# A two-layer transformer on one core: expert results stored by indirect transfers in token order, and cross attention reordered

## The reference, cut to what matters

```python
x = x + ga * _L0_attn_ref(layernorm(x) * (1 + ca) + sa)
x = x + gb * _L0_ffn_ref(layernorm(x) * (1 + cb) + sb)      # 8 experts, top 2
x = x + ga * _L1_attn_ref(...)                              # 16 heads of 8
x = x + gb * _L1_ffn_ref(...)     # cross attention over the batches, then 8 experts, top 2
...
scores = jnp.einsum('sbhd,tbhd->bhst', q, k) * scale        # s, t: 4 batches
attn = jnp.einsum('bhst,tbhd->sbhd', jax.nn.softmax(jnp.where(causal, scores, ...)), v)
...
expert_out = jnp.einsum('etf,efh->eth', gelu(jnp.einsum('th,ehf->etf', x, moe_w1)), moe_w2)
moe_out = jnp.einsum('eth,et->th', expert_out, weights)     # weights: 0 but for the best 2
```

## Time and profile before

| what | us |
|---|---|
| median of 3 runs (2000.09 to 2002.37) | 2000.48 |
| the profiled execution, its own time | 1998.0 |
| span of the profile, first to last instruction | 1996.2 |
| busy: PE, DVE, ACT, POOL | 1524.6, 1306.7, 1121.0, 544.4 |

### The profile page before, as it was taken

One profiled execution on the slowest core, in us unless ns is written; L12 is line 12 of the kernel. 1 busy time (PEld: TensorE's weight loads), 2 busy tenths in 40 slices (PEclk: granted clock), 3 DMA queues, 4 the chain that ended last, 5 costly groups with the idle time before them and its releaser, 6 DMA issues. The chain is left out here.

```text
span 1996.2 us, 36212 instructions
## 1 busy us (share of the span) xinstructions
PE 1524.6 (76%) x12536; PEld 846.8 (42%) x12536; DVE 1306.7 (65%) x3285; ACT 1121.0 (56%) x2869; POOL 544.4 (27%) x614
## 2 busy tenths in 40 slices
PE   6799999999924994338999999999999635414910
PEld 3377777777724994221222222222222324414910
DVE  5655656666651321669999999999999268833423
ACT  3377777777712442343888888888888533201300
POOL 1143334536255003731001001001000020471056
PEclk8799999999966997666999999999999957556955
DMA  6155212112105772340000000000000000014822
GB/s 207 38 175 182 88 32 52 42 39 56 32 28 169 228 228 86 90 134 17 23 20 25 19 27 19 27 18 27 18 19 2 1 6 1 22 51 137 263 80 71
DMA packets 86208, 139.61 MB, mean 70 GB/s; under 512 B 18084, under 2 KB 57252, under 8 KB 85772
## 3 DMA queue, kind: packets, MB, share of 16 engines
q1 hardware_dynamic: 62860, 92.60, 15.7%
q0 software_dynamic: 11936, 34.49, 5.2%
q10 hardware_dynamic: 11232, 10.23, 1.5%
HBM read 76.03 MB, written 45.11 MB: 61 GB/s over the span
## 5 line engine op out<-in xcount | busy, mean ns | idle before, releaser
L2064 DVE TENSOR_REDUCE q_max<-s_ps 128x1 f32<-128x1024 f32 x512 | 597.8, 1217 | 14.2 <-PE s_ps L1955 6.5
L2045 ACT ACTIVATE probs<-s_ps 128x512 f32<-128x512 f32 x1024 | 535.5, 603 | 124.4 <-PE s_ps L1976 124.2
L1955 PE MATMUL s_ps<-k_stack,q_stack 64*128 64x512 bf16 x1024 | 351.4, 396 | 17.0 <-PEq L97 8.6
L1976 PE MATMUL s_ps<-q_stack,k_stack 64*128 64x512 bf16 x1024 | 319.6, 384 | 20.1 <-ACT probs L2045 15.7
L1990 PE MATMUL o_ps<-probs,v_aug 128*32 128x512 f32 x2048 | 273.6, 606 | 0.7 <-ACT probs L2045 0.7
L1976 PEld LDWEIGHTS s_ps<-q_stack,k_stack 64*128 64x128 bf16 x1024 | 78.4, 94 | 334.5 <-ACT probs L2045 282.4
L873 ACT ACTIVATE probs<-s_biased,s_min 128x128 f32<-128x128 f32 x512 | 198.8, 391 | 15.8 <-DVE s_min L962 14.5
L991 POOL TENSOR_TENSOR probs<-probs,p_rsum 128x512 f32<-128x512 f32 x128 | 132.7, 1037 | 270.3 <-DVE p_rsum L968 269.8
L962 DVE CUSTOM_DVE_ANT_0 s_biased<-score_ps,nbias 128x128 f32<-128x128 f32 x512 | 117.7, 285 | 48.9 <-PE score_ps L738 37.1
L1582 POOL CAST neg_max_parts<-neg_max 16x128 bf16<-16x128 f32 x32 | 9.0, 281 | 474.6 <-DVE neg_max L2072 474.6
L974 DVE COPY probsT<-probsT_ps 128x512 f32<-128x512 f32 x128 | 86.9, 679 | 71.4 <-PE probsT_ps L750 71.4
(11 more groups left out here) (313 smaller groups left out, 2683.6 us busy)
## 6 DMA issues: line engine op xcount, KB each, us to landing
moe0b_wblock<-in_L_ffn_blocks SPq DMA_DIRECT2D x39, 578.0 KB, 4.1
moe_rows<-zero_rows POOLq DMA_DIRECT2D x18, 960.0 KB, 4.8
moe1b_wblock<-in_L_ffn_blocks SPq DMA_DIRECT2D x39, 256.0 KB, 3.6
v_shift<-v_tiles SPq DMA_DIRECT2D x32, 256.0 KB
v_shift<-v_tiles SPq DMA_DIRECT2D x32, 224.0 KB
qk_parts_dram<-qk_parts SPq DMA_DIRECT2D x16, 384.0 KB, 2.7
q_stack<-qk_parts_dram SPq DMA_DIRECT2D x192, 32.0 KB
k_stack<-qk_parts_dram SPq DMA_DIRECT2D x192, 32.0 KB
```

What stands on the lines that cost most here:

```text
L1955: mm = nc.tensor.matmul(s1[u % 2][:, c * CH:(c + 1) * CH], qs[head_rows(m), quad % 4, j, qt * P:(qt + 1) * P], ks[head_rows(m), quad % 4, ...
L1976: nc.tensor.matmul(bank_of("exp", 4 * k + pos)[:], ks[head_rows(m), quad % 4, j, kt * P:(kt + 1) * P], qs[head_rows(m), quad % 4, j, half ...
L2045: nc.scalar.activation(pr[:, k % 2, HEADS[pos], :], bank_of("exp", n)[:], ACT.Exp).then_inc(sm["exp"], 1)
L2064: v.tensor_reduce(mx[:, h % 4, col:col + 1], s1[u % 2][:], AX.X, ALU.max).then_inc(sm["maxed"], 1)
```

## The change

Four things are changed.

1. **Tags.** A row that is scattered now has 130 elements: the 128 features, the token's number (t+1)/4096, and the first row of the span of its first expert (`tag`, three small DVE instructions a batch, in `choose`). Each layer has its own `moe_rows`, both cleared during window attention: 36 transfers on POOL's queue in place of 18.
2. **Results in token order.** In `block_stage` DVE works out from the two tags where each row of a block belongs (`destinations`, three instructions of 128x2): the token's place in the first or second half of a new tensor `moe_y`, or a spare row for an empty one. POOL stores a block's results with two indirect transfers of 128 rows each, in place of ACT's plain one. SP loads a table of spare rows at the stage's start. `destinations(j)` waits until the results of block j-8 are stored.
3. **Plain loads.** Both combining stages load the results from `moe_y` in 16 plain transfers of 256 KB, by SP, and in the last stage by SP and ACT together; POOL's 128 indirect fetches are gone. In the last stage the first product moves from DVE to ACT. In `gather_qkv_stage` four loads stand ahead of the weights on SP's queue and twelve behind them.
4. **Cross attention.** The seven products of batches 2 and 3 go to POOL, before and between deviations 0 and 1. The order on DVE, ACT and PE goes by batch, so that batch 0's `place` stands ahead of `weighted(2)` and `finish(2)`. On POOL the scatter of batch b stands ahead of deviation b+2.

```diff
+TAGS = 2
+RW = D + TAGS
+SPARE = 2 * B * T + 1
+YROWS = SPARE + B * T + NBK * BR
...
-                    if g % 2 == 1 and g // 2 < FILLS:
+                    if g % 2 == 1 and g // 2 < 2 * FILLS:
...
+    def tag(self, dve, rows, b):
+        v, ts = self.nc.vector, slice(b * TPB, (b + 1) * TPB)
+        v.tensor_copy(rows[:, ts, D], self.token[:, ts])
+        self.step(dve, v.tensor_tensor(self.picked[:, 0], self.hot[:, 0], bc(self.steps[:, 0:E], 1, TPB), ALU.mult))
+        self.step(dve, v.tensor_reduce(rows[:, ts, D + 1], self.picked[:, 0], AX.X, ALU.add))
...
# block_stage
+                for j in range(NBK):
+                    pool.wait_ge(to_set, j + 1)
+                    pool.wait_ge(y_out, j + 1)
+                    for a in range(H):
+                        nc.gpsimd.indirect_dma_start(
+                            K.moe_y, bass.IndirectOffsetOnAxis(ap=to[:, j % YB, a:a + 1], axis=0), ys[:, j % YB, a, :], None
+                        ).then_inc(stored[j % YB], 16)
+                for i in range(YB):
+                    pool.wait_ge(stored[i], 16 * H * len(range(i, NBK, YB)))
...
+                sp.dma_start(spare[:].rearrange("p j a -> p (j a)"), K.A["spare"]).then_inc(spare_in, 16)
...
-                    act.wait_ge(y_out, k + 1)
-                    act.dma_start(K.moe_rows[bass.ds(rows.pop(k), BR), :].rearrange("(p a) d -> p a d", a=H),
-                                  ys[:, k % YB]).then_inc(stored[k % YB], 16)
...
+                def destinations(j):
+                    dve.wait_ge(x_in[j % XB], 16 * (j // XB + 1))
+                    if j >= YB:
+                        dve.wait_ge(stored[j % YB], 16 * H * (j // YB))
+                    if j == 0:
+                        dve.wait_ge(spare_in, 16)
+                    token, top = xi[:, j % XB, :, D], xi[:, j % XB, :, D + 1]
+                    v.scalar_tensor_tensor(out=empty[:, j % 2], in0=token, scalar=0.0, in1=spare[:, j, :],
+                                           op0=ALU.is_equal, op1=ALU.mult).then_inc(tested, 1)
+                    v.scalar_tensor_tensor(out=second[:, j % 2], in0=top, scalar=M.first_row[:, j:j + 1], in1=token,
+                                           op0=ALU.not_equal, op1=ALU.add).then_inc(tested, 1)
+                    dve.wait_ge(tested, 2 * (j + 1))
+                    v.scalar_tensor_tensor(out=to[:, j % YB], in0=second[:, j % 2], scalar=float(B * T),
+                                           in1=empty[:, j % 2], op0=ALU.mult, op1=ALU.add).then_inc(to_set, 1)
...
                     if j + 1 < NBK:
                         tokens_out(j + 1)
+                    if j < NBK:
+                        destinations(j)
                     if j >= 1:
                         rows_out(j - 1)
...
+def load_results(K, eng, yg, c, choice):
+    row = 1 + choice * B * T + c * CH
+    return eng.dma_start(yg[:, c * CPT:(c + 1) * CPT, choice, :],
+                         K.moe_y[row:row + CH, :].rearrange("(t p) d -> p t d", p=P))
...
# gather_stage
-                for t in range(NT):
-                    for c in range(2):
-                        nc.gpsimd.indirect_dma_start(
-                            yg[:, t, c, :], None, K.moe_rows, bass.IndirectOffsetOnAxis(ap=M.slot[:, c, t:t + 1], axis=0)
-                        ).then_inc(got[t // CPT], 16)
+            @block.scalar
+            def _(act):
+                for c in range(NCH):
+                    load_results(K, act, yg, c, 1).then_inc(got[c], 16)
+                for c in range(NCH):
+                    act.wait_ge(got[c], 32)
+                    if c >= 2:
+                        act.wait_ge(added, c - 1)
+                    for i in range(CPT):
+                        t = c * CPT + i
+                        nc.scalar.activation(u[:, c % 2, i, :], yg[:, t, 0, :], ACT.Copy, scale=M.weight[:, 0, t:t + 1]
+                                             ).then_inc(first, 1)
...
# gather_qkv_stage, SP
+                for c in range(2):
+                    for choice in range(2):
+                        load_results(K, sp, yg, c, choice).then_inc(got[c], 16)
                 for i, n in enumerate(("L1_attn_WqT", "L1_attn_WkT", "L1_attn_WvT")):
...
+                for c in range(2, NCH):
+                    for choice in range(2):
+                        load_results(K, sp, yg, c, choice).then_inc(got[c], 16)
...
# cross_route_stage, POOL
+                for n in range(5):
+                    early_product(n)
                 N.deviation(pool, 0)
+                early_product(5)
+                early_product(6)
                 N.deviation(pool, 1)
+                M.scatter(pool, N, 0, 0, TPB)
                 N.deviation(pool, 2)
-                M.scatter(pool, N, 0, 0, TPB)
+                M.scatter(pool, N, 1, 0, TPB)
                 N.deviation(pool, 3)
-                for b in range(1, B):
-                    M.scatter(pool, N, b, 0, TPB)
+                M.scatter(pool, N, 2, 0, TPB)
+                M.scatter(pool, N, 3, 0, TPB)
...
# cross_route_stage, the order on DVE after the change
+                scores(0); scores(1); shares(0); weighted(0, 0, 1); shares(1); weighted(1, 0, 2); finish(0)
+                scores(2); N.normalised_odd(dve, 0); finish(1); scores(3); N.normalised_odd(dve, 1)
+                M.shift_logits(dve, 0); M.choose(dve, N, 0); shares(2); M.place(dve, 0); weighted(2, 0, 3)
+                M.shift_logits(dve, 1); M.choose(dve, N, 1); shares(3); M.place(dve, 1); finish(2)
+                weighted(3, 0, 2); N.normalised_odd(dve, 2); weighted(3, 2, 4)
+                M.shift_logits(dve, 2); M.choose(dve, N, 2); finish(3); M.place(dve, 2)
+                N.normalised_odd(dve, 3); M.shift_logits(dve, 3); M.choose(dve, N, 3); M.place(dve, 3); M.tabulate(dve)
```

More of the change, by code:

```diff
@@ L939, in routed @@
                         M.weights(dve, b)
+                        M.tag(dve, N2.rows, b)
                     elif at == PREFIX + 1:
@@ L1272, in choose @@
         self.weights(dve, b)
+        self.tag(dve, N.rows, b)
     def place(self, dve, b, before=None):
@@ L1408, in _ @@
                                  ).then_inc(w_in[j % WBUF], 16)
-                for i in range(YB):
-                    sp.wait_ge(stored[i], 16 * len(range(i, NBK, YB)))
+                sp.wait_ge(spare_in, 16)
             @block.tensor
@@ L1477, in _ @@
                                              ).then_inc(g_out, 1)
-                for k in range(NBK - 3, NBK):
-                    store(k)
             @block.vector
@@ L1547, in _ @@
                 for c in range(NCH):
-                    dve.wait_ge(got[c], 16 * 2 * CPT)
-                    if c >= 2:
-                        dve.wait_ge(added, c - 1)
-                    for i in range(CPT):
-                        t = c * CPT + i
-                        v.tensor_scalar(u[:, c % 2, i, :], yg[:, t, 0, :], M.weight[:, 0, t:t + 1], None, ALU.mult
-                                        ).then_inc(first, 1)
+                    dve.wait_ge(got[c], 32)
                     for i in range(CPT):
@@ L1566, in _ @@
                     v.tensor_tensor(h, h, u[:, c % 2], ALU.add).then_inc(added, 1)
-            if out is not None:
-                @block.sync
-                def _(sp):
+            @block.sync
+            def _(sp):
+                for c in range(NCH):
+                    load_results(K, sp, yg, c, 0).then_inc(got[c], 16)
+                if out is not None:
                     for c in range(NCH):
@@ L2193, in cross_route_stage @@
         pd = K.sb("x_prod", [P, 2, TPB, QW], ctx=st)
+        early = [(s, t) for s in (2, 3) for t in range(s + 1)]
+        ep = K.sb("x_early_prod", [P, len(early), TPB, QW], ctx=st)
         at = K.sb("x_attended", [P, 2, TPB, QW], ctx=st)
@@ L2403, in weighted @@
                     step(v.tensor_tensor(row, row, bc(mx[:, s, :], 1, s + 1), ALU.mult))
+                def weighted(s, begin, end):
+                    f = first[s]
                     a = at[:, s % 2]
-                    if s >= 2:
+                    if s >= 2 and begin == 0:
                         dve.wait_ge(turned, 2 * (s - 1))
-                    for t in range(s + 1):
+                    for t in range(begin, end):
                         weight = bc(sc[:, f + t, :].rearrange("p (m r) -> p m r", r=R), 3, HD1)
```

209 lines of the change are left out of this document (110 added, 99 removed).

## The result

The changed kernel takes 1956.53 us (median of 4 runs, 1954.94 to 1957.03) against 2000.28 of the kernel before: a ratio of 0.978, 95% interval 0.9765 to 0.9796. That is 44 us less, where 61 were forecast; it lies 1.5 us above the upper end of the range. The profiled execution took 1954.94, its span 1953.1.

What follows compares the result with a forecast made beforehand. No engine was taken to bound the whole; POOL's indirect fetches, 1.29 us each, bound the last stage's chain. Terms summed to -61.1 us from the profiled 1998.0, so 1936.9; plus 2.5 for the median, 1939 us, range 1920 to 1955.

Steps and rivals of the forecast that it cites:

- the ends of the two block stages: Exits after the last indirect stores: layer 0 blocks +2.9 us in all; layer 1 landing 1.6 and 0.7 to enter.
- the start of the last stage: Last combination, -59.6 us in all: first chunk's loads 1.9, landing 2.0, then 0.7 until DVE begins.
- Layer 1 blocks becoming POOL-bound: Layer 1 blocks, +23.7 us: POOL needs 2 x 1.29 a block against PE's 1.98 and sets the pace.
- Cross attention: Reordered stage with seven products on POOL, -6 us: batch 0's slots at 1709.5 instead of 1716.76; bounds -16.5 and +2.
- The hold: Cross attention: DVE's two-input work is held beside POOL's products, 7 x 1.5 = 10.5 us; bounds 0 and 16.6.
- no hold: Rival, chance 0.25: POOL's products do not hold DVE, cross attention gains 16.5 us, slots at 1699, total 1929.
- Combination with the projections: Stage after the layer 0 blocks, -24.7 us: first norm at 16.9 instead of 35.7, waits before later norms gone.
- Window attention: 18 more clears on POOL, +1.0 us, bounds 0 and 3.3; tags separately +0.7, from batch 3's scatter moving.
- The bounds: Whole sum: all terms at their low bounds give about 1917 us, all at their high ones 1974.
- Dearer POOL work: Rival, chance 0.16: layer 1 block pitch 1.40 (+8.6 us) and products of 3 to 4 us (+6), total 1954.
- Slower than before: Rival, chance 0.03: indirect stores back up beside the blocks' loads, POOL's pitch over 1.93 us in both block stages.
- the loads do not pay: Rival, chance 0.01: plain loads under 60 GB/s keep the last stage near 80 us, total about 1996.

Runs made afterwards that it cites:

- e1: The changed kernel without the first of POOL's drains at the exit of both block stages, waits for landing kept: 1943.97 us.
- e2: The changed kernel with half of layer 1's results left out, so 39 indirect stores there instead of 78: 1934.89 us (one run).
- e5: The changed kernel with one more POOL drain in both block stages, ahead of block 20's stores: 1956.19 us (one run).
- e7: The kernel before the change, without POOL's first drain at the exit of layer 0 routing and cross attention: 1993.09 us against 2001.44.
- e4: The changed kernel with all 16 loads of the last stage issued by SP and none by ACT: 1952.10 us.
- e8: As e3, but POOL also makes its seven products, into a buffer that nobody reads: 1964.77 us (one run).
- e3: The changed kernel with all ten cross attention products on DVE, in the changed order, none on POOL: 1954.59 us.
- e10: The changed kernel with the 18 clears of layer 1's rows issued during full attention instead of window attention: 1990.88 us.

## Why the prediction was wrong, by its own steps

The direction, the mechanisms and six of nine pieces held (within 1.5 us); two steps, which stand in the other three pieces, were too short by more than the range had room for.

- *The failed step: the ends of the two block stages.* I wrote "POOL ends at about 777.3, lands by 778.9, and the next stage starts near 779.8", and for layer 1 "landing 1.6 and 0.7 to enter the next stage". From POOL's end to the next stage that is 2.5 and 2.3 us; measured were 8.9 and 8.9, of which 6.42 are the drain, a term that the sum does not have. I priced the exit of a stage whose POOL has issued 78 indirect transfers by that of a stage that ends with a plain store (773.91 to 776.94 in the earlier trace rows). e1 gives 12.6 us for the two, and without the drain its exits are the 2.4 and 2.5 us that I had; e2 and e5 show how the price scales. The trace of before had it: 1806.68 to 1816.97 after 64 scatters, 10.3 us, of which e7 takes 5.3 away. Moving indirect transfers from inside a stage to its end moves this price onto the path; I counted the transfers and not what they leave behind.
- *The second mis-sized term: the start of the last stage.* "1.9 us and 2.0 for landing; 0.7 until ACT's products let DVE begin", 4.6 in all; measured 8.8. The part that I left out is ACT's issuing of its own eight loads, 8.24 us ahead of the first product. e4 returns 4.4 us. Eight chunks took 20.1 us of DVE, forecast 20.8.
- *Layer 1 blocks becoming POOL-bound:* right. 78 stores take 98.6 us from 1812.75 to 1911.32, a pitch of 1.264, forecast 1.29 (2.0 us better), and POOL begins 1.2 us later after the first rows than I had it. The excess of 5.8 us is 6.6 (exit) - 2.0 + 1.2. DVE waits nine times for a landing there, in `destinations`; but POOL's stores follow one another 0.30 us apart, and e2 shows that their number sets the pace:

```profile
DVE moe1b_empty L1522 <- DMA moe_y<-moe1b_y,moe1b_to: 12.4, 9, 2.9
```

- *Cross attention:* right, and for the stated reason. The hold was priced at 10.5, as 1.5 us for each of seven products, from L921's 0.15 us and the one-input share; the stretched instructions of the changed kernel make 10.5, and e8 against e3 measures 9.65. That the total agrees so closely is in part luck: the first three products cost 4.0 us, the next two 4.0 and the last two 2.5, not 1.5 each. The slots came at 65.6 us, which is 1708.2 by the old count, forecast 1709.5. The rival "no hold" (1699) is refuted. The Trainium skill's rule on this pair (SBUF — State Buffer, section Who interferes with whom) has both sides of this, and the trace agrees: 0.42 becomes 2.44 us with two inputs, 0.94 stays with one.
- *Combination with the projections:* right to 0.5 us; the first norm came at 18.2 us, forecast 16.9.
- *Window attention:* 1.0 was forecast, 3.5 came (from POOL's first softmax product to its last, 460.7 before by its line's last numbers, 464.2 after; and a start about 1 us earlier hides a part of it in the table). I put only batch 3's tag on the path. In the trace POOL's softmax products fall behind in five steps, three of 0.6 (one tag each) and two of 0.87; e10 removes 1.7 us with the clears.
- *The bounds.* Those that the terms state add up to about 1923 and 1963, not to the 1917 and 1974 of the text. The measured time lies inside either pair and outside the narrower range.
- *The rivals.* "Dearer POOL work" gave 1954, near the result, by another mechanism: the pitch was cheaper than forecast, and the products took the 2.4 us assumed. "Slower than before" and "the loads do not pay" are refuted by a pitch of 1.264 and a last stage of 32.9 us.

## What to carry to other kernels

Read the exit of a stage as a row of its own: where a stage ends with POOL's indirect transfers, look at the gap to the next stage's first instruction in a stage that already ends so, and price a moved transfer with what it adds there (here 0.083 us each). Work moved to POOL beside DVE is priced by the two-input instructions of DVE that it will meet, and an engine that issues loads ahead of its own work pays for the issuing first. A stretch in which the transfer engines are 7% busy is not free for large transfers, if short ones there stand on the path.

## What the runs showed of the hardware that I had not expected

- The drain's price goes with the number of indirect transfers since the last drain: without it an exit takes 2.4 us, landing included (e1); 39 transfers add 3.3 us (e2), 78 add 6.5. Its own records are 2.67, 3.16, 3.24, 5.27 and 6.42 us after 32, 38, 39, 64 and 78 transfers of 128 rows, 0.082 to 0.083 us for each. It does not return in the drains that follow in the same barrier, and all stores had long landed: in the changed kernel the transfers end by 1912.5, the next stage begins at 1920.24.
- The hold works both ways: POOL's root of 128x8 takes 2.54 us beside DVE's product in e3 and 1.64 in the changed kernel, where one-input sums run beside it. The first scatter after the slots, which begins inside a product of DVE, takes 1.79 us; the next three, which begin as one ends, take 0.96.
- Full attention moves 21 GB/s and was still slowed by 33 us through 18 clears, which is 1.8 us for each.
